# Moving a gate bank under the left product, and ScalarE's keys into PSUM, in a two-layer attention and experts kernel

## The reference

```python
# attention, A = 64 features, N = 512 tokens per batch entry, 4 entries
q, k = xn @ Wq.T, xn @ Wk.T
e = relu(sqrt(relu(q_i + k_j) + 1e-8) - sqrt(relu(-(q_i + k_j)) + 1e-8))   # [N, N, A]
scores = e @ Wphi;  ex = exp(scores - max);  denom = sum(ex)
out = (ex @ Vy + (sum_j ex_ij * e_ija) @ We.T + We_b * denom) / (denom + 1e-9)
# experts, 8 of them, DFF = 256, each computed for all tokens and weighted by its share
z = (xn @ w1 + b1) * (xn @ w2 + b2)
y = silu(z @ wg + bg) @ w3 + b3
```

## Time and profile before

| | |
|---|---|
| runs, us | 1397.66 median of 3 (1397.62, 1397.66, 1400.98) |
| profiled execution, us | 1398.52 |
| its span, us | 1396.8, mean granted clock 0.976 |
| busy: PE, PEld | 1212.3 (87%), 579.2 (41%) |
| busy: DVE, ACT, POOL | 1212.8 (87%), 1135.3 (81%), 892.1 (64%) |
| chain that ended last | DVE 36%, PE 31%, issue 5%, ACT 1% |
| reductions L1051 | 1024, 677 ns each; idle before them 68.7 us, 67.6 for PE ps L1341 |
| roots L1188 | 128, 3707 ns each |
| ScalarE's features L1176 | 330, 712 ns each; idle before them 45.2 us, all for DVE L1051 |
| VectorE's features L1037 | 214, 580 ns each |
| broadcasts L1341 | from 429.3 to 1384.7 us |

### The profile page before, as it was taken

One profiled execution on the slowest core, in us unless ns is written; L12 is line 12 of the kernel. 1 busy time (PEld: TensorE's weight loads), 2 busy tenths in 40 slices (PEclk: granted clock), 3 DMA queues, 4 the chain that ended last, 5 costly groups with the idle time before them and its releaser, 6 DMA issues.

```text
span 1396.8 us, 21175 instructions
## 1 busy us (share of the span) xinstructions
PE 1212.3 (87%) x6185; PEld 579.2 (41%) x6185; DVE 1212.8 (87%) x3409; ACT 1135.3 (81%) x1292; POOL 892.1 (64%) x1294
## 2 busy tenths in 40 slices
PE   3899999997737989998989998989998889998887
PEld 2577767675512333333333333333333333333333
DVE  5777888887658999999998999998999999999997
ACT  1776888885258999989999989999999999998950
POOL 0754733332004888888888878888888888888820
PEclk9999999999668999999999999999999999999999
DMA  6001100000000000010000010000000000001001
GB/s 191 9 11 26 28 1 0 0 1 1 19 0 16 20 19 19 20 31 27 20 20 20 20 31 20 27 20 20 20 23 27 27 20 19 19 20 31 27 20 34
DMA packets 38843, 32.36 MB, mean 23 GB/s; under 512 B 6150, under 2 KB 35609, under 8 KB 38738
## 3 DMA queue, kind: packets, MB, share of 16 engines
q1 hardware_dynamic: 37714, 29.76, 7.3%
q0 software_dynamic: 1024, 1.35, 0.6%
HBM read 29.10 MB, written 2.75 MB: 23 GB/s over the span
## 4 chain that ended last, share of the span: by engine, by line
DVE 36%; PE 31%; issue 5%; ACT 1%; DVEq 0%; ACTq 0%
DVE arena L1051 22%; PE ps L1328 10%; PE ps L1341 9%; DVE arena L1037 6%; PE ps L1405 4%; PE ps L1385 4%; DVE s L1083 3%; DVE x L1094 2%; PE ps L1377 2%; PE ps L1359 2%; DVE spread L1103 2%; DVE nmax L1043 1%; ACT arena L1188 1%; PE ps L1363 0%; DVE shift L1045 0%
## 5 line engine op out<-in xcount | busy, mean ns | idle before, releaser
L1051 DVE SCALAR_TENSOR_TENSOR arena<-arena,ps 128x512 f32<-128x512 f32 x1024 | 663.7, 677 | 68.7 <-PE ps L1341 67.6
L1188 ACT ACTIVATE arena<-arena,eps 128x4096 f32<-128x4096 f32 x128 | 474.1, 3707 | 6.0 <-ACT arena L1176 5.7
L1305 POOL TENSOR_SCALAR arena<-kT,negq 128x512 f32<-128x512 f32 x480 | 345.1, 725 | 179.2 <-DVE arena L1051 170.0
L1341 PE MATMUL ps<-spread,sel 128*128 128x512 f16 x1024 | 357.3, 386 | 100.5 <-DVE arena L1051 94.4
L1311 POOL TENSOR_SCALAR arena<-arena,q 128x512 f32<-128x512 f32 x480 | 349.4, 739 | 22.4
L1341 PEld LDWEIGHTS ps<-spread,sel 128*128 128x128 f16 x1024 | 91.8, 97 | 492.2 <-DVE arena L1051 377.5
L1328 PE MATMUL ps<-arena,phi_cols 128*32 128x512 f32 x2048 | 274.5, 610 | 20.6 <-ACT arena L1188 20.6
L1176 ACT ACTIVATE arena<-kT,q 128x512 f32<-128x512 f32 x330 | 216.9, 712 | 45.2 <-DVE arena L1051 45.2
L462 POOL TENSOR_SCALAR kT<-kT,region 128x512 f32<-128x512 f32 x128 | 89.3, 698 | 155.2 <-DVE region L587 154.6
L512 ACT ACTIVATE kT<-ps,region 128x512 f32<-128x512 f32 x128 | 88.1, 688 | 59.3 <-DVE region L582 57.8
L1392 PE MATMUL ps<-z,wge 128*128 128x512 f32 x256 | 130.8, 592 | 0.3 <-DVE z L1077 0.3
(11 more groups left out here) (196 smaller groups left out, 1720.8 us busy)
## 6 DMA issues: line engine op xcount, KB each, us to landing
wge<-in_e_wg SPq DMA_DIRECT2D x32, 256.0 KB, 2.7
w1e<-in_e_w SPq DMA_DIRECT2D x32, 128.0 KB, 2.1
w2e<-in_e_w SPq DMA_DIRECT2D x32, 128.0 KB, 2.1
w3e<-in_e_w SPq DMA_DIRECT2D x32, 128.0 KB, 2.2
region<-in_w SPq DMA_DIRECT2D x1, 2048.0 KB
out<-x SPq DMA_DIRECT2D x4, 256.0 KB, 2.9
region<-in_wqk SPq DMA_DIRECT2D x1, 512.0 KB, 4.7
region<-in_wv SPq DMA_DIRECT2D x1, 512.0 KB, 5.4
```

Source lines behind the costliest of these rows:

```text
L1051: dve.scalar_tensor_tensor(feat[:, j, k, :], feat[:, j, k, :], 1.0, psB[:, k % BANKS, :], ALU.mult, ALU.mult, accum_out=sums[:, j, gg, c:c ...
L1188: act.activation(grp, grp, ACT.Sqrt, bias=eps[:]).then_inc(e_ready, 2)
L1305: pool.tensor_scalar(feat[:, j, QUADS * gg + c, :], kT[:, b * N:(b + 1) * N], HUGE, negq[:, b % 2, at - b * N // 2:at - b * N // 2 + 1], A ...
L1341: pe.matmul(psB[:, k % BANKS, :], sel[:, gg, c, :], spread[:, j, :], start=True, stop=True).then_inc(bc_done, 1)
```

## The change

Bank 1 no longer takes half 0 of the gate. ScalarE copies the keys of a batch entry into it (at m = 2, 8, 16, 24) and reads its features' keys from there. Gate half 0 is written into psY, the bank of the left product and of the experts' output, so it is made after half 1, when the output of the slot before has been added, and the left product of half 0 comes after the silu of half 0. The steps that this moves: TensorE's `left_product(m, 0)` from (6,3) to (0,1) of its own slot and `left_product(m, 1)` from (0,3) to (1,0); the gate from (3,3), (4,1), (4,3), (5,1) to (3,3), (4,1), (5,2), (6,0), half 1 first; VectorE's additions from (5,0), (5,2), (5,3) to (4,2), (4,3), (5,0); the copy of the left product on ScalarE from its group 7 to its group 0. VectorE makes 3 features per slot and ScalarE 13: groups 0 and 3 change hands. ScalarE's wait for `bg_halved` goes to its first tanh. In the last slot gate, silu and additions come earlier, and the down product is made at (7,1) and (7,2).

```diff
-    ON_DVE = [1, 0, 1, 1, 0, 1, 1, 0]
+    ON_DVE = [0, 0, 1, 0, 0, 1, 1, 0]
...
-        psX, psY, psZ = ps[:, 6, :], ps[:, 7, :], ps[:, 1, :]
-
-        b3_banks = (psX, psY, psZ, psO)
+        psX, psY, psK = ps[:, 6, :], ps[:, 7, :], ps[:, 1, :]
+        psG = (psY, psX)
+
+        b3_banks = (psX, psY, ps[:, 2, :], psO)
...
                 def silu(m, f):
-                    dve.wait_ge(lifted, m * GT + f + 1)
-                    dve.scalar_tensor_tensor(s[:, f, :], (psZ, psX)[f], ...
+                    dve.wait_ge(lifted, m * GT + 2 - f)
+                    dve.scalar_tensor_tensor(s[:, f, :], psG[f], ...
...
-                            (4, 1): lambda: final or largest(m + 1, 1 - j),
-                            (5, 0): lambda: none or add_experts(m - 1, 1),
-                            (5, 2): lambda: none or add_experts(m - 1, 2),
-                            (5, 3): lambda: none or add_experts(m - 1, 3),
-                            SILU_AT[0]: lambda: silu(m, 0),
-                            SILU_AT[1]: lambda: silu(m, 1),
+                            **({} if final else {(4, 1): lambda: largest(m + 1, 1 - j)}),
+                            **({(4, 1): lambda: add_experts(m - 1, 1), (4, 2): lambda: add_experts(m - 1, 2),
+                                (4, 3): lambda: add_experts(m - 1, 3)} if final else
+                               {(4, 2): lambda: none or add_experts(m - 1, 1),
+                                (4, 3): lambda: none or add_experts(m - 1, 2),
+                                (5, 0): lambda: none or add_experts(m - 1, 3)}),
+                            **({(5, 1): lambda: silu(m, 1), (6, 0): lambda: silu(m, 0)} if final else
+                               {SILU_AT[0]: lambda: silu(m, 1), SILU_AT[1]: lambda: silu(m, 0)}),
...
                 def features(m, j, gg):
                     b, pair0 = slot_parts(m)
+                    if gg == 0 and (m == 2 or m % BB == 0):
+                        if m > 2:
+                            act.wait_ge(act_feat, (m - 2) * sum(ON_ACT))
+                        act.activation(psK, kT[:, b * N:(b + 1) * N], ACT.Copy).then_inc(k_copied, 1)
+                        act.wait_ge(k_copied, b + 1)
...
-                        act.activation(feat[:, j, QUADS * gg + c, :], kT[:, bass.ds(b * N, N)], ACT.Relu,
+                        act.activation(feat[:, j, QUADS * gg + c, :], psK, ACT.Relu,
...
                 def tanh_half(m, first=False):
                     if not first:
                         act.wait_ge(y_done, m)
-                    for f in range(GT):
-                        act.wait_ge(gate_done, m * GT + f + 1)
+                    else:
+                        act.wait_ge(bg_halved, 1)
+                    for n, f in enumerate((1, 0)):
+                        act.wait_ge(gate_done, m * GT + n + 1)
...
-                            if gg == LEFT_AT[0] and not (last and j == 1):
-                                keep_left(m + 1, 0)
+                            if gg == 0 and not none:
+                                keep_left(m, 0)
...
-                act.wait_ge(bg_halved, 1)
                 for n in range(2 * GROUPS):
...
                 def lift(m):
-                    for f in range(GT):
-                        pool.wait_ge(tanh_ready, m * GT + f + 1)
+                    for n, f in enumerate((1, 0)):
+                        pool.wait_ge(tanh_ready, m * GT + n + 1)
...
                 def left_product(m, f, first=0):
                         if first < 2:
                             pe.wait_ge(left_kept, m * GT)
+                            pe.wait_ge(s_ready, m * GT)
...
                 def gate(m, f, half):
-                    if half == 0 and f == 0:
+                    if half == 0 and f == 1:
                         pe.wait_ge(z_ready, (m + 1) * GT)
                         pe.wait_ge(wg_in, (m + 1) * 16)
-                    ins = pe.matmul((psZ, psX)[f], ...
+                    if half == 0 and f == 0 and m:
+                        pe.wait_ge(y_added, m * TB)
+                    ins = pe.matmul(psG[f], ...
...
-                            (0, 3): lambda: left_product(m, 1),
+                            (0, 1): lambda: none or left_product(m, 0, first=1 if m == 1 else 0),
+                            (1, 0): lambda: left_product(m, 1),
...
-                            (3, 3): lambda: gate(m, 0, 0),
-                            (4, 1): lambda: gate(m, 0, 1),
-                            (4, 3): lambda: gate(m, 1, 0),
-                            (5, 1): lambda: gate(m, 1, 1),
+                            (3, 3): lambda: gate(m, 1, 0),
+                            (4, 1) if not final else (4, 0): lambda: gate(m, 1, 1),
+                            (5, 2) if not final else (5, 0): lambda: gate(m, 0, 0),
+                            (6, 0) if not final else (5, 1): lambda: gate(m, 0, 1),
                             (6, 1): lambda: transpose_ex(m, j, none),
-                            (6, 3): lambda: final or left_product(m + 1, 0, first=1 if none else 0),
+                            **({(7, 1): lambda: down(m, 0, last=True), (7, 2): lambda: down(m, 1)} if final else {}),
...
                 tile(NT - 1, last=True)
-                down(MB - 1, 0, last=True)
-                down(MB - 1, 1)
                 combine(MB - 1, 1, 0)
```

More of the change, by code:

```diff
@@ L988, in second_layer @@
         act_passed = sem("act_passed")
+        k_copied = sem("k_copied")
         lifted, bg_halved = sem("lifted"), sem("bg_halved")
@@ L1080, in silu @@
                 def silu(m, f):
-                    dve.wait_ge(lifted, m * GT + f + 1)
-                    dve.scalar_tensor_tensor(s[:, f, :], (psZ, psX)[f], bg[:, f, bass.ds(m % E, 1)], s[:, f, :],
+                    dve.wait_ge(lifted, m * GT + 2 - f)
+                    dve.scalar_tensor_tensor(s[:, f, :], psG[f], bg[:, f, bass.ds(m % E, 1)], s[:, f, :],
                                              ALU.add, ALU.mult).then_inc(s_ready, 1)
@@ L1221, in tanh_half @@
                         act.wait_ge(y_done, m)
-                    for f in range(GT):
-                        act.wait_ge(gate_done, m * GT + f + 1)
+                    else:
+                        act.wait_ge(bg_halved, 1)
+                    for n, f in enumerate((1, 0)):
+                        act.wait_ge(gate_done, m * GT + n + 1)
                         act.sem_inc(act_passed, 1)
-                        act.activation(s[:, f, :], (psZ, psX)[f], ACT.Tanh, bias=bgh[:, f, bass.ds(m % E, 1)],
+                        act.activation(s[:, f, :], psG[f], ACT.Tanh, bias=bgh[:, f, bass.ds(m % E, 1)],
                                        scale=0.5).then_inc(tanh_ready, 1)
@@ L1388, in gate @@
                 def gate(m, f, half):
-                    if half == 0 and f == 0:
+                    if half == 0 and f == 1:
                         pe.wait_ge(z_ready, (m + 1) * GT)
                         pe.wait_ge(wg_in, (m + 1) * 16)
-                    ins = pe.matmul((psZ, psX)[f], wg[:, half * DFF + f * P:half * DFF + (f + 1) * P], z[:, half, :],
+                    if half == 0 and f == 0 and m:
+                        pe.wait_ge(y_added, m * TB)
+                    ins = pe.matmul(psG[f], wg[:, half * DFF + f * P:half * DFF + (f + 1) * P], z[:, half, :],
                                     start=(half == 0), stop=(half == 1))
@@ L1420, in tile @@
                             (3, 1): lambda: none or down(m - 1, 1),
-                            (3, 3): lambda: gate(m, 0, 0),
-                            (4, 1): lambda: gate(m, 0, 1),
-                            (4, 3): lambda: gate(m, 1, 0),
-                            (5, 1): lambda: gate(m, 1, 1),
+                            (3, 3): lambda: gate(m, 1, 0),
+                            (4, 1) if not final else (4, 0): lambda: gate(m, 1, 1),
+                            (5, 2) if not final else (5, 0): lambda: gate(m, 0, 0),
+                            (6, 0) if not final else (5, 1): lambda: gate(m, 0, 1),
                             (6, 1): lambda: transpose_ex(m, j, none),
-                            (6, 3): lambda: final or left_product(m + 1, 0, first=1 if none else 0),
-                            (0, 2): lambda: none or right_product(m, 0),
+                            **({(7, 1): lambda: down(m, 0, last=True), (7, 2): lambda: down(m, 1)} if final else {}),
+                                                        (0, 2): lambda: none or right_product(m, 0),
                         }
```

## The result

The change makes the kernel slower: 1505.4 us in the median of three runs (1502.07 to 1507.13) against 1397.66, a ratio of 1.0759 with a 95% interval of 1.0721 to 1.0797. The forecast was 1453 with a range of 1400 to 1475. The direction was right, the size was not.

The account below looks back on a forecast made before the run. No engine alone bounded the slot: the path alternated between VectorE and TensorE, ScalarE's roots 1.1 us from it. Slots +68, key copies +1, start -12.3, end -2.2 and +0.9 gave +55.4 us: 1453 against the median, range 1400 to 1475.

Parts of the forecast that it names:

- The loop: Per slot from reduction (3,3): late gate half delays ScalarE's tanh and roots, then TensorE's scores; 32.35 us for 30.08.
- 0.86 + 2 x 0.22 after a start at 5.55: TensorE's gate half and two broadcasts after the additions, in us from reduction (3,3); the last half starts at 6.85.
- The walk of the end: Last slot to kernel end: -2.2 us for the earlier down product, +0.9 for the extra product at the slot's head.
- -2.2: Kernel end: with the down product ahead of the last broadcasts, the combination starts at 1388.4 instead of 1390.7, 2.2 us less.
- The left product at the head: Left product (m, 0) at (0,1), in TensorE's own stretch: 0.86 us more per slot, bounds 0 to 0.95.
- another 0.1: ScalarE's last root, behind the copy of left product (m, 1), ends near 26.0 where TensorE is at 25.9: 0.1 us.
- VectorE's feature of group 3: At (4,2), on VectorE's part of the path: taking it away saves 0.46 us per slot.
- A: Rival: only TensorE's stretch grows, ScalarE is in time; +0.4 to +0.9 a slot, 1397 to 1412 us; chance 0.14.
- B: Rival: TensorE catches up at the slot's head and VectorE's load decides; faster, 1349 or 1371 us; chance 0.12.
- C: Rival: collisions go, the feature at (3,2) costs 0.46 and not 0.83; 12 us less, 1441; chance 0.1.
- E: Rival: the wait at the start does not shorten, bias products hold the first slot; +12 us, 1465; chance 0.05.
- D: Rival: ScalarE's features cost as before and late-root scores at (7,3) push the next slot; 1468 to 1477 us; chance 0.08.

Follow-up runs that it names:

- early_adds: Changed kernel with VectorE's four additions all at (3,3) and gate half 0 at (4,3) and (5,1): 1415.78 us, a slot 31.08.
- filler: Changed kernel with 12 extra 128x512 matmuls per slot in TensorE's gaps ahead of gate half 0, results unused: 1467.88 us.
- down_at_end: filler with the last down product back behind the last slot: 1464.38 us.
- left_head: Kernel before with only the two left products and ScalarE's copy of the first moved to (0,1) and (1,0): 1428.6 us, a slot 31.10 to 31.12.
- one_feature: start_wait with VectorE's feature of group 3 given to ScalarE, all features from SBUF, no bank shared: 1371.61 us, ratio 0.9822.
- dve_features_filler: filler with VectorE's five features per slot back (ScalarE makes 11, from PSUM): 1491.93 us, most slots 33.52.
- start_wait: Kernel before with only ScalarE's wait for the halved bias moved from the first roots to the first tanh: 1387.66 us, ratio 0.9923.
- no_tanh_wait: Changed kernel with ScalarE's second tanh made from gate half 1, so it does not wait for half 0 (wrong result): 1505.06 us.

## Why the prediction was wrong

The loop was right: additions, gate half, tanh, table, two roots, scores, TensorE's stretch. Each step lies within 0.2 us of its forecast place in the short slots, and a slot there takes 32.66 for 32.35. Over 28 passages these 0.3 us are about the 7 us by which the passages at full clock exceed the forecast. That the late gate half is the cause was tested: with it early the tanh's wait and the long slots are gone (early_adds). Two small slips of the walk change nothing: its terms add up to 32.32 and not 32.35, and the scores of group 4 come 1.28 late by its own rows (19.35 for 854.82 - 836.75), not 1.23.

The step that failed is "0.86 + 2 x 0.22 after a start at 5.55". It priced the gate half and its broadcasts at the upper clock, because the clock of both stretches was 1.00. But the change itself put in front of the gate a stretch in which TensorE mostly waits (0.83 us busy of 2.5). In 17 of 30 passages the clock fell there and the slot took 2.2 us more, in three more some 1.35; filler shows it, 39 us of the 52 that were missing. The rest is the 7 us above and 4 us at the end of the kernel. The page of the kernel before had the sign; these are its rows of TensorE's busy tenths and of the clock:

```profile
PE   3899999997737989998989998989998889998887
...
PEclk9999999999668999999999999999999999999999
```

The clock has 6, 6 and 8 in the slices in which TensorE is busy for 7, 3 and 7 tenths, at the start of the second layer. I read 1.00 in the slot and did not ask what the new wait would do to it.

The walk of the end failed too, +2.8 for a forecast of -1.3. The extra product at the head of the last slot was right: the first gate part stands 24.7 us after the last maximum in down_at_end and 23.9 before (1373.97 - 1350.03), 0.8 for 0.9, with the clock low in parts of both. "-2.2" for the earlier down product was wrong: left at the end it would have cost 0.44 us, since its silu comes earlier too, and moved forward it ran at the lower clock and delayed the last two reductions. The lower clock in the last slot is in no term of the forecast.

The two terms that were tested alone held. The left product at the head costs 1.02 (left_head) for 0.86 and the walk's "another 0.1" at the last root. VectorE's feature of group 3 is worth 0.44 for 0.46 in the kernel before (one_feature); in the changed kernel, put back with its neighbour, it costs 0.84 at the held clock (dve_features_filler), where the one at (4,2) holds VectorE for 0.87. So a price read in one schedule did not carry over to another.

The rivals: A (ScalarE in time) is excluded by 2.9 and 5.1 us of tanh wait; B (TensorE has room at the head of the slot) by left_head; C by the feature at (3,2), still 0.90 long at 806.47; E by start_wait. D named a late root at (7,3) as the push; TensorE does wait 1.74 us there in the short slot, but the excess came from the clock.

What stays open: why the clock falls in two slots of three when the idle time ahead of the gate is the same in all (5.60 from R to the gate in both kinds); how much of a slot the sharing of the bank costs by itself; and why one instruction of VectorE has two durations.

## What to carry to other kernels

A wait that a change adds to TensorE has two prices: the wait, and the time at the lower clock of whatever follows it; price both, by rows at either level. Before trading a PSUM bank for a cheaper operand, ask whether the work can move without it: here moving one feature and one wait, with no bank shared, gave 1.8% (one_feature), while every kernel tried here that shared the bank was slower than the kernel before. When a move of work makes another step early, ask again what the old place still costs: the down product at the end had stopped costing 2.2 us. And when an experiment takes away one suspected wait and nothing changes, look at the clock before believing it.

## What the runs showed of the hardware that was not expected

- Twelve extra matmuls a slot made the kernel 39 us faster, with the granted clock at 1.00 from 560 to 1340 (filler). The clock of the changed kernel had fallen to 0.50 although no single wait of TensorE ahead of it was longer than 1.00 us; five waits of 0.22 to 1.00 us lie between 840.7 and 845.6.
- Removing a wait left the time unchanged, 1505, since the clock then fell in 29 of 30 passages: 0.908 in the mean for 0.937 (no_tanh_wait).
- The same VectorE feature, 128x512 from SBUF to SBUF, holds the engine 0.46 us at (4,2) of the kernel before and 0.87 at (4,2) of dve_features_filler.
- A Relu of 128x512 on ScalarE takes 682 ns from PSUM (mean of 390, the changed kernel) and 712 from SBUF (mean of 330, the kernel before).
